# Attention and mixture-of-experts layer: the first head pair's operand rows come straight from a projection with repeated columns, and chunks 0 and 1 are projected among the maxima

## What is computed

```python
xn = _layernorm(x)
q, k, v = (split_heads(xn @ W + b) for W, b in ((Wq, bq), (Wk, bk), (Wv, bv)))
weights = softmax(q @ k.T / sqrt(8))            # per head, 1024 x 1024
attn = (weights @ v) @ Wo + bo
logits = xn @ router_w.T; top 2 experts per token, sigmoid gates
ffn = sum over experts of gate * (silu(xn @ w_gate[e]) * (xn @ w_up[e])) @ w_down[e]
out = x + attn + ffn
```

## Time and profile before

| | |
|---|---|
| runs | 868.89, 870.05, 873.38 us; median 870.05 |
| the profiled execution | 869.59 us, of which the span from the first to the last instruction is 867.9 |
| busy in the span | PE 819.4 us (94%), DVE 740.4 (85%), ACT 694.4 (80%), POOL 471.3 (54%) |
| mean granted TensorE clock | 0.972 of full |

### The profile page before, as it was taken

The page is one execution under the profiler, slowest core; times in us unless marked ns, Lnnn a source line. Parts: engine busy times, 40 slices in busy tenths (PEclk is TensorE's granted clock), DMA queues, the critical chain, the costliest instruction groups (busy, mean ns, idle before and its releaser), DMA issues.

```text
span 867.9 us, 20181 instructions
## 1 busy us (share of the span) xinstructions
PE 819.4 (94%) x6725; PEld 446.6 (51%) x6725; DVE 740.4 (85%) x1380; ACT 694.4 (80%) x1521; POOL 471.3 (54%) x670
## 2 busy tenths in 40 slices
PE   8996767789999999999999999999999999999997
PEld 7762222335555555555555555555555555555533
DVE  6579998999888978989989888988888888898834
ACT  3453645579898988989989898888998988898885
POOL 3442008024576756767667656766666756666410
PEclk9996877999999999999999999999999999999999
DMA  4678077022343333333443433333334343332133
GB/s 119 173 238 263 5 151 49 15 65 69 91 92 90 82 80 80 72 98 75 100 93 89 100 82 87 86 77 91 84 75 99 80 99 95 87 96 61 39 91 111
DMA packets 94952, 80.92 MB, mean 93 GB/s; under 512 B 19560, under 2 KB 84320, under 8 KB 94816
## 3 DMA queue, kind: packets, MB, share of 16 engines
q1 hardware_dynamic: 80336, 67.51, 29.9%
q0 software_dynamic: 13632, 11.79, 9.1%
q10 hardware_dynamic: 880, 0.33, 0.3%
HBM read 57.99 MB, written 22.71 MB: 93 GB/s over the span
## 4 chain that ended last, share of the span: by engine, by line
PE 81%; DVE 13%; ACT 2%; issue 2%; DMA 2%; SPq 1%; ACTq 0%; DVEq 0%
PE ps L1176 27%; PE ps L1161 17%; PE ps L1151 15%; PE ps L1223 7%; DVE maxima L957 6%; PE ps L1206 6%; PE ps L1189 2%; ACT probs L667 1%; PE ps L1063 1%; DVE xnT L943 1%; PE ps L1212 1%; PE ps L1239 1%; PE ps L1183 1%; DMA gu_w<-L_ffn_w_up 1%; DVE stage L934 1%
## 5 line engine op out<-in xcount | busy, mean ns | idle before, releaser
L957 DVE TENSOR_REDUCE maxima<-ps 128x1 f32<-128x512 f32 x1024 | 638.5, 684 | 74.7 <-PE ps L1161 69.8
L667 ACT ACTIVATE probs<-ps 128x512 f32<-128x512 f32 x1024 | 537.9, 610 | 107.5 <-PE ps L1151 103.9
L1161 PE MATMUL ps<-qk 64*128 64x512 f32 x1024 | 392.5, 441 | 36.2 <-DVE maxima L957 34.0
L1151 PE MATMUL ps<-qk 64*128 64x512 f32 x1024 | 381.9, 462 | 2.2 <-ACT probs L667 1.9
L1161 PEld LDWEIGHTS ps<-qk 64*128 64x128 f32 x1024 | 183.8, 188 | 175.0 <-DVE maxima L957 142.9
L1176 PE MATMUL ps<-probs,v_all 128*9 128x512 f32 x2048 | 271.8, 603 | 1.7 <-ACT o_sb L673 1.1
L1151 PEld LDWEIGHTS ps<-qk 64*128 64x128 f32 x1024 | 179.8, 188 | 23.8 <-ACT probs L667 14.9
L565 POOL DMA_INDIRECT acc<-result,idx x71 | 117.6, 1656 | 114.5 <-issue 93.9
L1223 PE MATMUL ps<-xg_T,gu_w 64*128 64x128 f32 x1136 | 155.4, 276 | 0.1
L1223 PEld LDWEIGHTS ps<-xg_T,gu_w 64*128 64x128 f32 x1136 | 145.6, 187 | 9.2 <-ACT result L694 9.0
L1206 PEld LDWEIGHTS ps<-dn_w,hid 64*128 64x128 f32 x568 | 74.4, 186 | 62.4 <-ACT probs L667 51.5
(11 more groups left out here) (152 smaller groups left out, 608.9 us busy)
## 6 DMA issues: line engine op xcount, KB each, us to landing
gu_w<-L_ffn_w_gate SPq DMA_DIRECT2D x71, 128.0 KB
gu_w<-L_ffn_w_up SPq DMA_DIRECT2D x71, 128.0 KB
dn_w<-L_ffn_w_down SPq DMA_DIRECT2D x71, 128.0 KB
qk<-q_parts SPq DMA_DIRECT2D x124, 64.0 KB
qk<-k_parts SPq DMA_DIRECT2D x124, 64.0 KB
k_parts<-stage SPq DMA_DIRECT2D x24, 256.0 KB, 3.5
q_parts<-stage SPq DMA_DIRECT2D x16, 256.0 KB, 3.5
x_sb<-L_attn_inputs SPq DMA_DIRECT2D x4, 512.0 KB, 8.9
```

The source lines that it names most:

```text
L667: act.activation(probs[:, u % NPB, q, h, :], ps[:, BANK_OF[job], :], ACT.Exp).then_inc(s_read, 1)
L957: dve.tensor_reduce(maxima[:, p % 2, qt, h, k:k + 1], ps[:, x_bank(i), :], AX.X, ALU.max, negate=True).then_inc(x_read, 1)
L1151: pe.matmul(ps[:, bank, :], t[r, 1, kt * P:(kt + 1) * P], t[r, 0, q * CH:(q + 1) * CH], start=True, stop=True).then_inc(s_filled, 1)
L1161: pe.matmul(ps[:, bank, :], t[r, 0, qt * P:(qt + 1) * P], t[r, 1, k * CH:(k + 1) * CH], start=True, stop=True).then_inc(x_filled, 1)
```

## The change

The 16 copies, the idle matmuls behind the first projections (`BRIDGE`) and the fills are gone. In their place:

- A weight tile `w_rows` holds, for the q and the k side, the first two heads' columns of Wq or Wk four times each, and zeros for the pad rows (VectorE zeroes it, ScalarE spreads the columns: `spread_weights`). Four projections with it, `FIRST_ROWS`, give the first pair's 128 rows for chunks 0 and 1 directly. ScalarE takes each out of PSUM twice (`take_rows_of_first`: the value, and the value times a 0/1 column that says whether the row is a low one), and VectorE makes the high part and combines both (`rows_of_first`). The biases of these rows come by four small DMAs of ACT into `row_bias`.
- `q` and `k` of chunks 0 and 1 go to slots 0 to 3, their logits to slots 4 and 5, their `v` to slots 18 and 19. All jobs of chunks 2 to 7 stand three slots later. SP stores chunks 0 and 1 and loads pairs 1 and 2 inside the unit loop. The last 8 tiles' statistics and the moments of chunks 2 to 7 stand on VectorE behind the maxima of u = -12 (`rest_moments`), their reciprocal behind those of u = -11 (`rest_rstd`).

```diff
+FIRST_ROWS = (("rows_q", 0), ("rows_k", 0), ("rows_k", 1), ("rows_q", 1))
 
 CHUNK_AT = {}
+SLOTS = [("q", 0), ("k", 0), ("q", 1), ("k", 1), ("lg", 0), ("lg", 1)]
+SLOT_OF = {job: n for n, job in enumerate(SLOTS)} | {("v", 0): 18, ("v", 1): 19}
 for _c in REST:
-    for _job, _slot in (("turn", 2 * _c - 1), ("lg", 2 * _c), ("q", 3 * _c - 1), ("k", 3 * _c), ("v", 3 * _c + 1)):
-        CHUNK_AT.setdefault((_slot // 2 - LX, 2 * (_slot % 2)), []).append((_job, _c))
-FILL_AT = [(_slot // 2 - LX, 2 * (_slot % 2)) for _slot in range(3)]
+    SLOT_OF |= {("turn", _c): 2 * _c + 2, ("lg", _c): 2 * _c + 3, ("q", _c): 3 * _c + 2, ("k", _c): 3 * _c + 3, ("v", _c): 3 * _c + 4}
+for _job, _slot in sorted(SLOT_OF.items(), key=lambda item: item[1]):
+    CHUNK_AT.setdefault((_slot // 2 - LX, 2 * (_slot % 2)), []).append(_job)
 UPPER_AT = {u: c for (u, n), jobs in CHUNK_AT.items() for job, c in jobs if job == "k"}
-LOGITS_AT = NC - 1 - LX
+LOGITS_AT = (2 * (NC - 1) + 3) // 2 - LX
...
+            act.wait_ge(sign_step, 2)
+            for z, b in enumerate((bq, bk)):
+                for h in range(2):
+                    act.dma_start(row_bias[64 * h:64 * h + 32, 0, z:z + 1],
+                                  b[D * h:D * h + D].rearrange("(a d e) -> a d e", a=1, e=1).broadcast_to([4, D, 1])).then_inc(rows_bias, 16)
             act.dma_start(rw_in[:, :], router_w).then_inc(small_in, 16)
             act.dma_start(bo_row[:, :], bo.rearrange("(a e) -> a e", a=1).broadcast_to([P, E])).then_inc(small_in, 16)
             act.dma_start(wo[:, :], Wo).then_inc(wo_in, 16)
...
+                    if c == 1:
+                        root(1)
+                        norm(2)
...
+            def take_rows_of_first(job, c):
+                z = ("rows_q", "rows_k").index(job)
+                act.wait_ge(s_filled, s_full(job, c))
+                act.activation(probs[:, c, z, 0, :], ps[:, BANK_OF[job, c], :], ACT.Identity, bias=row_bias[:, 0, z:z + 1],
+                               scale=(SCALE, 1.0)[z])
+                act.activation(probs[:, c, z, 1, :], ps[:, BANK_OF[job, c], :], ACT.Identity, bias=row_bias[:, 1, z:z + 1],
+                               scale=row_scale[:, z:z + 1]).then_inc(s_read, 1)
+
             root(0)
+            act.wait_ge(proj_in, 48)
+            act.wait_ge(rows_w, 1)
+            for z in range(2):
+                spread_weights(z)
             act.wait_ge(rw_T, 1)
             act.activation(rw_cols[:, :], ps[:, 7, 0:NE], ACT.Copy).then_inc(rw_ready, 1)
             take_turn(0)
             take_turn(1)
...
-            act.wait_ge(const_step, NE + 2)
...
+            act.wait_ge(const_step, NE + 4)
+            for job in FIRST_ROWS:
+                take_rows_of_first(*job)
...
+            dve.memset(w_rows[:, :, :, :, :], 0.0).then_inc(rows_w, 1)
+            for z in range(2):
+                dve.memset(row_bias[:, 0, z:z + 1], float(z)).then_inc(sign_step, 1)
...
+            dve.wait_ge(rows_bias, 16 * 4)
+            dve.tensor_scalar(row_bias[:, 0, 0:1], row_bias[:, 0, 0:1], SCALE, None, ALU.mult).then_inc(const_step, 1)
+            dve.wait_ge(const_step, NE + 3)
+            dve.wait_ge(sign_step, 8)
+            dve.tensor_tensor(row_bias[:, 1, :], row_bias[:, 0, :], is_lo[:, :], ALU.mult).then_inc(const_step, 1)
...
             statistics(2)
-            upper(0)
-            upper(1)
-            statistics(3)
-            dve.wait_ge(stat_done, NT)
-            rest = slice(NT // B, NT)
-            moments(rest)
-            dve.wait_ge(std_ready, 2)
-            dve.reciprocal(mom[:, 1, rest], mom[:, 4, rest]).then_inc(rstd_ready, 1)
-            dve.wait_ge(rstd_ready, 1)
-            dve.scalar_tensor_tensor(mom[:, 5, rest], mom[:, 0, rest], -1.0, mom[:, 1, rest], ALU.mult, ALU.mult).then_inc(rstd_ready, 1)
             dve.wait_ge(small_in, 16 * 2)
             dve.wait_ge(bo_ps, 1)
             dve.tensor_tensor(bo_row[:, :], bo_row[:, :], ps[:, 5, 0:E], ALU.add).then_inc(bo_ready, 1)
+
+            def rows_of_first(n, job, c):
+                z = ("rows_q", "rows_k").index(job)
+                dve.wait_ge(s_read, s_taken(job, c))
+                all_of, lo_of = probs[:, c, z, 0, :], probs[:, c, z, 1, :]
+                dve.tensor_scalar(all_of.bitcast(I32), all_of.bitcast(I32), TOP, None, ALU.bitwise_and).then_inc(sign_step, 1)
+                dve.wait_ge(sign_step, 8 + n + 1)
+                dve.scalar_tensor_tensor(qk[0][:, z, c * CH:(c + 1) * CH], all_of, row_sign[:, z:z + 1], lo_of,
+                                         ALU.mult, ALU.add).then_inc(pair_ready, 1)
...
+                    if UPPER_AT[u] == 0:
+                        rest_moments()
+                    if UPPER_AT[u] == 1:
+                        rest_rstd()
                 if u == 0:
                     dve.wait_ge(lg_ready, 1)
-                    dve.wait_ge(filled_up, 1)
...
             pe.wait_ge(wo_in, 16)
             pe.wait_ge(bv_ready, 1)
             pe.matmul(ps[:, 5, 0:E], bv_bc[:, :], wo[:, :], start=True, stop=True).then_inc(bo_ps, 1)
-            for _ in range(BRIDGE):
-                pe.matmul(ps[:, 6, 0:P], ident[:, :], ident[:, :], start=True, stop=True)
...
+            pe.wait_ge(rows_w, 3)
+            for job, c in FIRST_ROWS:
+                z = ("rows_q", "rows_k").index(job)
+                project(job, c, w_rows[:, z].rearrange("p h n d -> p (h n d)"))
+            pe.wait_ge(rw_ready, 1)
...
+                if p == 0:
+                    pe.wait_ge(pair_ready, 4 if qt >= TPC else 3 if k == 1 else 2)
```

130 lines of the change are left out of this document (54 added, 76 removed).

## The result

The changed kernel takes **882.16 us** (median of 4 runs, 881.93 to 883.66), beside 869.94 for the kernel before in the same comparison. The ratio is 1.0144, with a 95% interval of 1.0120 to 1.0168: slower by 1.4%. Its profiled execution took 882.07 us, of which 880.3 are the span.

The account below looks back on a forecast made before the run. TensorE bounds from 29.4 to 66.3 us, then VectorE to 170. Terms -0.1 (routing start), +0.7 (clock), +0.7 and +1.4 (behind routing) sum to +2.7 on 869.6: 872.3 us, 8-in-10 range 865.8 to 876.4.

Parts of the forecast that it names:

- Step 1: Start: bias DMAs delay the row of bo, so TensorE's first transposes start at 12.5 us, not 10.13.
- A: VectorE's first max reduction, forecast at 23.5 us against 29.9 before.
- Step 2: From the first transposes through the four row projections to VectorE's first max reduction, forecast at 23.5 us.
- Step 3: VectorE's and ScalarE's chain before chunk 2 takes 12.1 us, so chunk 2's transposes start at 35.6, against 32.84.
- T: Start of chunk 2's transposes on TensorE, forecast at 35.6 us against 32.84 before.
- Step 5: TensorE idles about 4.3 us before chunk 2 and its clock falls; mostly hidden in waiting, +0.7 us (0 to 4).
- Step 4: Heavy slots from chunk 2's transposes to routing: TensorE bound, routing starts at 66.8 us, 0.1 earlier than before.
- the low clock lasts in the heavy slots: Rival, chance 0.18: TensorE stays cold for 8 of the 24 us of heavy slots, +4 us, total 876.
- Costed at nothing: Items expected to cost no time, among them GpSimd's pads moved between the `lower` calls, and later stores.
- Step 6: Behind routing's start: one more `upper` +0.7 us, and chunk jobs in u = 0 delaying reductions +1.4 us.
- M-R: Time from routing's start to the third step joining the maxima; forecast to grow 2.1 us.
- The lead is kept: Rival, chance 0.13: TensorE is not held before chunk 2, routing starts at about 62 us, total about 865.

Follow-up runs that it names:

- e11: Changed kernel with the four row bias loads behind Wo and VectorE's two row-bias products behind its second normalization; 880.38 us, ratio 1.0123.
- e7: Changed kernel with GpSimd's pads of pairs 1 to 3 all behind the low parts of chunk 1; 877.26 us, ratio 1.0104.
- e8: Changed kernel, start rebuilt: bias loads and pads moved, moments before the first reduction, chunk 2 earlier, v jobs later, two idle matmuls; 871.14 us, ratio 1.0027.
- e3: Changed kernel with idle matmuls in its thin slots and the pads of pairs 1 to 3 ahead of everything on GpSimd; 877.65 us, ratio 1.0104.
- e1: Changed kernel with idle matmuls where TensorE waits among the first maxima; 879.20 us, ratio 1.0128.
- e9: e8 with its gaps filled by more idle matmuls and the logits of chunks 0 and 1 moved back; 874.98 us, ratio 1.0071.
- e10: e9 with the pads spread, pair 1's beside the statistics; 873.13 us, ratio 1.0040.
- e12: e10 with idle matmuls cut to what the gaps hold and chunk 0's logits early again; 869.28 us, ratio 1.0008.

## Why the prediction was wrong

It gave 872.3 us with a range to 876.4; it came out at 882. Its own sum was 9.8 us short, point by point:

- **Step 1 held by two errors that offset** (11.94 against 12.5): bo_row was issued 0.95 us later than forecast, and landed some 1.9 sooner. The bias issues took 1.95 and 1.30 us, and bo_row's transposition began 5.2 us behind its issue at 6.70. Its price was not what it seemed: where e11 takes the wait away, the chunk transposes begin only 0.80 us earlier (11.29), released by the norm, and A doesn't move (e11's own row bias comes late as well, as said).
- **Step 2 was 2.0 us too long** (A = 21.52 against 23.5). Of these, 0.6 are step 1's; 1.2 lie between there and the first row projection, 2.2 us for the 3.4 assumed, since the transposes of both chunks ran without a gap; 0.2 lie behind. The combining instruction took 0.75, near the 0.69 assumed. All four row projections took 3.60 us together, so none was cold. That was the luck of this execution: e7, with the same program up to A, lost its clock at 13.5 us and has A = 23.15.
- **Step 3 held in VectorE's chain, and not in what TensorE does beside it** (T = 34.89 against 35.6). The chain ends with the normalization of chunk 2 on ScalarE, row below, at 34.32, 12.8 us behind A for the 12.1 forecast. In it the two instructions of 0.83 and 0.92 above took about 0.2 each in the kernel before, 1.4 us more together. The first runs beside `lower(0)` on GpSimd, the second beside `lower(1)`. e8 shows the chain by taking the moments away. The rest of the chain took 0.7 less than forecast. But T wasn't released by the normalization. TensorE waited 1.20 and 2.21 us (3.4 for the 4.3 of step 5), and from 29.15 on it was busy without a gap, with maxima and logits at the lower clock, up to the transposes of chunk 2. They began 0.6 us behind the end of the normalization. So at the lower clock its own work no longer "fits beside it", and the end of the slow time didn't fall into waiting.
- **Step 4 held** where nothing disturbs: from T to R it forecast 66.8 - 35.6 = 31.2, and e3 has 30.70.
- **Step 5 failed in its size, and it is the largest miss.** It put the clock at 0.7 us; the runs show 5.6 in R-T (after against e1), of which some 4.0 are the first low stretch and 1.6 a second one, which came only in traces with the pads at `upper(4)`. The step assumed that the slow time would fall into the waiting before chunk 2. The clock was lost at 24.3 us, behind short gaps, and came back only at 44.8, 9.9 us after the heavy slots had begun. The rival "the low clock lasts in the heavy slots" was the right mechanism (it named 8 us of cold work and 4 us), and had only 0.18.
- **"Costed at nothing" failed for GpSimd.** The prediction asked when pair 1 needs its pads, and not what VectorE does beside them. The pads cost 1.6 us in R-T by themselves (`upper(4)`) and 1.0 behind R (`upper(6)`); GpSimd's `lower` beside the moments about 1.4 in step 3, and beside `chosen` 0.9.
- **Step 6 was too small.** The forecast was 0.7 + 1.4. In M-R the kernel lost 6.69. Up to the second joining of the maxima (106.11, and 94.96 before) it is 5.26, and the rows name it: VectorE waits 0.64, 1.65 and 0.35 for maxima, and not at all before; one more `upper` 0.7; `upper(6)` 1.0 and `chosen` 0.9 longer; together 5.2. The first two waits stand in u = 0, where step 6 put them. The other 1.4 us come behind the second joining: from 127 to 145 us, where the mean clock is 0.59 against 0.71 in the like stretch of before, 1.6 us are lost. The prediction had nothing there, and what loses the clock there wasn't tested.

The sum of the misses: -2.0 (A), +1.3 (A to T), -0.5 (T to R undisturbed), +4.9 (clock: 5.6 for 0.7), +1.6 (pads, T to R), +4.6 (M-R: 6.7 for 2.1), -0.1 behind M, together 9.8. The terms T to R and the two behind it use e3's and e1's traces, one execution each.

ScalarE's DMA queue of the changed kernel, for step 1:

```profile
2.85 1.95 ACTq L576 DMA_DIRECT2D row_bias<-L_attn_bq  x2
4.83 1.30 ACTq L576 DMA_DIRECT2D row_bias<-L_attn_bk  x2
...
6.70 0.36 ACTq L579 DMA_DIRECT2D bo_row<-L_attn_bo  x1
```

And its ScalarE, for step 3:

```profile
32.67 1.65 ACT L592 ACTIVATE x_sb<-x_sb,mom 128x128 f32<-128x128 f32 x4 [4.00 <-DVE mom L869]
```

No store was late at `upper(4)`: VectorE shows no idle time before 61.13. "The lead is kept" fell with step 3, and e8, which removes step 3, is no faster than the kernel before either.

What stays open: why the clock falls in one execution and not in another on nearly the same rows (e9 and e10, the starts of e7 and the changed kernel, e1's and the changed kernel's `upper(4)`), and with that, where e12's slower runs lose.

## What to carry to other kernels

A first result that comes 10 us earlier is worth nothing if the engines behind it then have little to do: the thin stretch costs the matmul clock, and the price is paid by the dense stretch behind, several us at a time. When work moves on GpSimd, look at what VectorE does in the same microseconds, not only at who waits for the result. And compare kernels by a few fixed moments up to the last one behind which all take the same time; a two-by-two of experiments at such a moment separates causes that the totals hide. But each corner is one execution: check a difference against the rows that are to explain it. Here M-R fell by 2.6 with the pads gone, and the rows gave 1.0.

## What the runs showed of the hardware

- **GpSimd beside VectorE.** Two VectorE instructions of 0.75 us together took 2.29 us beside memsets of 1.03 each, four norms 2.42 instead of 1.11, a 128x24 addition 0.83 instead of 0.2; statistics (4.74 against 4.73) and reductions out of PSUM (2.48) were not touched. The Trainium skill (SBUF — State Buffer, Who interferes with whom) says that VectorE and GpSimd share one pair of ports, which one instruction holds until it ends while the other waits, and that only some forms of VectorE instruction need it. The rows agree: 1.54 us of delay for two instructions is within two memsets of 1.03.
- **The clock fell without a long gap**: at 24.3 us behind gaps of 0.57 and 1.20 us with TensorE busy in between, and at 65.3 behind one of 1.03; e1 kept it behind one of 1.04 at the same rows. It fell behind a gap of 2.09 us in e9, and not behind one of 1.99 in e10.
- **The clock stayed low under gapless work**: in the changed kernel TensorE has no gap from 29.15 us on (maxima, logits of 8 columns, transposes, two projections), and the lower level lasted until 44.8.
- **The same rows, another clock**: up to A the changed kernel and e7 have one program; the four row projections took 3.60 us in one execution and 4.61 in the other.
- **Idle matmuls have a price of their own when the clock has fallen**: eight cost 3.78 us in e1 and ten 3.44 in e9, against 2.39 for ten at full clock in e10.
- **DMA issues on ScalarE's queue**: two took 2.99 us in e11 and 1.95 in the changed kernel, beside 0.36 to 0.58 for one in the earlier trace rows.
